# Global attention's output projection moved into the attention block, with its first groups loaded ahead and x added by matmul

## The chip, the cores and the metric

The kernel runs on one core of one Trainium2 chip. The metric is the device time of one execution in microseconds (us), lower is better. The kernel before is stated as the median of three runs.

## What is computed

A modulated transformer block on x of 2 x 2048 tokens with 256 channels. What matters here is the first half:

```python
h = _layernorm(x) * (1 + ca) + sa
x = x + ga * (h + attention(h) @ Wo.T)        # 8 heads of 32, causal, two softmaxes mixed
h = _layernorm(x) * (1 + cb) + sb             # input of the second half
x = x + gb * ffn(h)                           # two layers of local attention and feed-forward
```

`ga`, `ca`, `sa` and the others are vectors of 256, one for each of the two batches. The kernel computes the second line as `h*ga + x + o @ (Wo*ga)`, where `o` is the heads' output.

## The kernel before

The program is a row of blocks. Each has a list of instructions for every engine, and all engines meet at its end. The blocks are: setup, the q, k and v projections, the global attention (`attention_phase`), the output projection (`projection_phase`), and then twice local attention and feed-forward. Before a block with new semaphores, `prime` (lines 106 to 117) makes a small block of its own in which SyncE alone adds 1 to every semaphore, one instruction for each.

`attention_phase` goes through 16 turns, one for each batch and head (`BH = 16`). The normalised and modulated `h` lies in SBUF as `S.h1`, which shares its memory with `x3` (the trace calls it `x`). In a turn TensorE makes score tiles, takes row maxima from a transposed copy and multiplies the two sets of probabilities with the values (L757), ScalarE makes the exponentials, and VectorE the second set's exponents (L859, L865) and maxima. What follows a head is a chain of small steps over DRAM, which for heads 0 to 14 runs inside the next turn: ScalarE copies the last product out (`keep`, L796), SyncE sends it and the row sums (`send`, L551 and L552) and loads the sums turned (`sums_load`, L567), VectorE inverts them (`invert`, L876 and L878), SyncE stores and loads the shares (L573, L580), GpSimd weighs and adds (`normalise`, L677 and L681), and SyncE stores the head's output to `o_t` (`o_store`, L586). For head 15 there is no next turn: the chain stands alone at the end of the block. Heads 0 to 7 belong to the first batch, 8 to 15 to the second.

`projection_phase` (from line 979) handles the 4096 tokens in 8 groups of 512 (`GROUPS = 8`, 4 tiles of 128 each); groups 0 to 3 are the first batch. For each group n:

- SyncE loads x (`fetch_x`, L1010, 512 KB) and the heads' outputs (`fetch_o`, L1014, two of 256 KB), and stores the new x (`send`, L1018).
- VectorE multiplies `h` by `ga` (`gate_x`, L1102), and GpSimd adds x to it (`add_x`, L1060).
- TensorE multiplies: 4 tiles by 2 halves of the channels, 8 matmuls of 256 columns, each recorded as two instructions (L1090), into one of two buffers of PSUM.
- VectorE adds the product (`residual`, L1110), takes mean and variance (L230, L235) and adds epsilon (L1115). GpSimd raises to -1/2 (`scale`, L1064), VectorE makes the offset (`centre`, L1120), ScalarE normalises (L1044), VectorE modulates (`modulate`, L1124), and GpSimd adds the shift into `x2` (`shift`, L1068), the input of the second half.

TensorE may begin group n only when `residual(n-2)` is done, since there are two buffers. After its second group ScalarE issues `W.load_local`: 11 transfers of the local attention's weights and tables, 5.9 MB (L964 to L968). The local attention block begins, as all blocks, when every engine is through.

Of the kernel before, what the change touches and what calls it, by code (L numbers as in the profile page):

```python
# [15 lines left out]
P = 128  # L16
# [81 lines left out]
def allocators(nc, ctx, sems, prefix=""):  # L98

    def sb(name, shape, dt=F32):  # L100
        return ctx.enter_context(nc.sbuf_tensor(prefix + name, shape, dt))

    def ps(name, shape, dt=F32):
        return ctx.enter_context(nc.psum_tensor(prefix + name, shape, dt))

    def sem(name):
        return sems.enter_context(nc.semaphore(prefix + name))

    return sb, ps, sem
# [348 lines left out]
def attention_phase(nc, S, io):  # L458
# [35 lines left out]
    with ExitStack() as ctx:  # L494
        sb, ps, sem = allocators(nc, ctx, S.sems)
        q3, k3 = ([sb(f"{n}{s}", [ALLROWS, T], F32R) for s in range(SETS)] for n in ("q3_", "k3_"))
        geo, kp_t = sb("geo_rows", [P, 2, T]), sb("kp_t", [P, NT, BH])
        vx = [sb(f"vx_{s}", [P, NT, VW]) for s in range(SETS)]
        chunk_max, row_max = sb("chunk_max", [P, NT, NG]), sb("row_max", [P, NT])
        max_parts = sb("max_parts", [P, 2 * NT], F32R)  # L500
        max_rows = [sb(f"max_rows{p}", [2 * n, P], F32R) for p, (_, n) in enumerate(PARTS)]
        probs = sb("probs", [P, PSLOTS, 2, GTOK])
        mask_n, mask_t = sb("mask_n", [P, P], BF16), sb("mask_t", [P, P], BF16)
        later = sb("later", [P, P])

        share = sb("share", [P, H])
        out_t = sb("out_t", [P, 2, GTOK])
        raw = [sb(f"raw_{s}", [P, 2, GTOK]) for s in range(SETS)]
        shares = sb("shares_in", [P, 2, GTOK])
        sums = sb("sums_in", [P, T * 2 // P])  # L510
        summed = sb("summed", [P, GTOK])

        piece_lo, piece_hi = sb("piece_lo", [P, PIECE], F32R), sb("piece_hi", [P, PIECE], F32R)

        dots = geo[0:BH, :, :]
        top, low = (probs[0:BH, 2 * k:2 * k + 2, :, :].rearrange("h s k t -> h (s k t)") for k in range(2))
        geo_x = sb("geo_x", [P, GSLOTS, GTOK])
        a_ps = ps("a_ps", [P, ABANKS, 512])
        st_ps = ps("st_ps", [P, STBANKS, 512])
        o_ps = ps("o_ps", [P, 2, 512])  # L520
        turned_ps = st_ps[:, 0, 0:NT * BH].rearrange("p (t h) -> p t h", h=BH)
        names = ("setup a_ready a_used parts_ready values_in max_in st_ready st_used geo_ready geo_link probs_ready pv_done o_used max_chain "
                 "inverted shared weighed summed sums_in shares_out shares_in o_out piece_hi piece_lo piece_out cleared dots_in kp_turned kp_kept chain rows_out").split()
        q = {n: sem("t_" + n) for n in names}

        masks_in, max_out, piece_in = sem("t_masks_in"), sem("t_max_out"), sem("t_piece_in")
        loads = [sem(f"t_load{s}") for s in range(SETS)]
        out_sent = [sem(f"t_out_sent{k}") for k in range(2)]
        geo_in = [sem(f"t_geo_in{g}") for g in range(NG)]
        SETUP, CHAIN = 2 * SETS + 1, 5  # L530
        LOAD, SENT, OUT = 16 * 6, 16 * 3, 16 * NG

        PROBS0, ST0, PV0, O0 = GSLOTS - 1, STBANKS - 1, PSLOTS - 1, 1

        prime(nc, q | dict(enumerate((*loads, *out_sent, *geo_in))), (("probs_ready", PROBS0), ("st_used", ST0), ("pv_done", PV0), ("o_used", O0)))

        def chunk(c):
            return slice(c * GTOK, (c + 1) * GTOK)

        with nc.Block() as block:  # L540

            @block.sync
            def _(sp):
                def send(b, g, s):
                    evens = SENT * (NG // 2) * (b + 1) + START
                    sp.wait_ge(q["o_used"], b * NG + g + 1 + O0 + START)
                    for kind in range(2):
                        if kind and g == NG - 1:

                            sp.wait_ge(out_sent[0], evens)  # L550
                        sp.dma_start(raw[s][g * D:(g + 1) * D, kind, :], out_t[kind * HALF:kind * HALF + D, g % 2, :]).then_inc(out_sent[g % 2], 16)  # L551
                    sp.dma_start(S.sums[ds(b, 1), :, chunk(g)].rearrange("h k t -> (h k) t"),  # L552
                                 out_t[D:D + HALF + 1:HALF, g % 2, :]).then_inc(out_sent[g % 2], 16)

                def geo_load(b, g):

                    sp.wait_ge(q["geo_ready"], (b - 1) * NB + last_of_group[g] + 1 + START)
                    geo_fetch(b, g)

                def geo_fetch(b, g):  # L560
                    sp.dma_start(geo[:, :, chunk(g)], S.geo[ds(b, 1), :, chunk(g)].to_broadcast([P, 2, GTOK])).then_inc(geo_in[g], 16)

                def sums_load(b):
                    flat = S.sums.rearrange("b k (p n) -> (b k p) n", p=HALF)
                    first, sent = b * P, SENT * (NG // 2) * (b + 1) + START
                    sp.wait_ge(out_sent[1], sent)
                    sp.dma_start(sums[:, :], flat[ds(first, P), :]).then_inc(q["sums_in"], 16)  # L567

                def shares_store(b):
                    flat = S.shares.rearrange("b k (p n) -> (b k p) n", p=HALF)  # L570
                    first = b * P
                    sp.wait_ge(q["shared"], b + 1 + START)
                    sp.dma_start(flat[ds(first, P), :], sums[:, :]).then_inc(q["shares_out"], 16)  # L573

                def shares_load(b):
                    flat = S.shares.rearrange("b k (p n) -> (b k p) n", p=HALF)
                    first = b * P
                    sp.wait_ge(q["shares_out"], 16 * (b + 1) + START)
                    for g in range(NG):
                        sp.dma_start(shares[g * D:(g + 1) * D, :, :], flat[ds(first, P), :].rearrange("(k g p) n -> g k (p n)", k=2, g=NG)[g:g + 1].to_broadcast([D, 2, GTOK])).then_inc(q["shares_in"], 16)  # L580

                def o_store(b):
                    first = [b // H * (NG * H) + b % H + g * H for g in range(NG)]
                    sp.wait_ge(q["summed"], b + 1 + START)
                    for g in range(NG):
                        sp.dma_start(S.o_t[ds(first[g], 1), :, :].rearrange("h d t -> (h d) t"),  # L586
                                     summed[g * D:(g + 1) * D, :]).then_inc(q["o_out"], 16)
# [1381 lines left out]
```

## Time and profile before

| | |
|---|---|
| median of 3 runs | 2828.08 us (2824.79 to 2835.54) |
| the profiled execution | 2834.22 us, its span 2832.1 us |
| PE busy | 2550.9 us (90%) |
| DVE busy | 2193.7 us (77%) |
| ACT busy | 1558.2 us (55%) |
| POOL busy | 562.9 us (20%) |
| DMA | 204.92 MB, mean 72 GB/s |

PE is TensorE's matmuls, DVE VectorE, ACT ScalarE, POOL GpSimd and SP SyncE. Busy time is an average over all stages. The page also cuts the span into 40 slices of 70.8 us; in slices 17 and 18, which hold the end of the global attention and the projection, PE is busy for four and seven tenths, and nine nearly everywhere in the attention around them. What a change between two stages is worth is to be read from the instructions of that stretch in order of time.

### The profile page before, as it was taken

What the parts mean: (1) busy time and instruction counts of PE and PEld (TensorE: products, weight loads), DVE (VectorE), ACT (ScalarE), POOL (GpSimd) and SP (SyncE); (2) the same over time, 40 slices, a digit from 0 to 9 for tenths busy, and PEclk for the clock granted to TensorE, in tenths of its full rate; (3) what the DMA queues carried; (4) which work ended last, traced back from release to release, by engine and by line L of the source; (5) the groups of instructions that cost most, each with busy time, mean ns of one, the idle gap of its engine ahead of it and who ended that gap; (6) DMA issues with size and microseconds to landing.
All of it is one profiled execution on the core that took longest, in us unless ns stands there. A gap on an engine that the chain in (4) does not pass through costs nothing. (4 is left out here: it accounts for less than half of the span.)

```text
span 2832.1 us, 45352 instructions
## 1 busy us (share of the span) xinstructions
PE 2550.9 (90%) x14072; PEld 1543.8 (55%) x14072; DVE 2193.7 (77%) x4594; ACT 1558.2 (55%) x3447; POOL 562.9 (20%) x388
## 2 busy tenths in 40 slices
PE   4995999999999999954799999979979999997998
PEld 2443433333333333313577777758867777775877
DVE  4776999999999999957688888745657888885665
ACT  0221666676667666642466666634426666665443
POOL 0110011011111010116333333300013333331000
PEclk7997899999999999987799999989989999999999
DMA  2334254454554444417200000030020000001121
GB/s 87 113 113 123 79 143 125 106 132 115 132 137 117 116 122 126 114 52 253 63 10 9 8 9 9 17 121 21 12 56 10 9 8 9 9 20 34 49 65 40
DMA packets 123906, 204.92 MB, mean 72 GB/s; under 512 B 22560, under 2 KB 71008, under 8 KB 120400
## 3 DMA queue, kind: packets, MB, share of 16 engines
q1 hardware_dynamic: 109040, 163.96, 21.1%
q0 software_dynamic: 8832, 21.80, 2.7%
q10 hardware_dynamic: 5920, 17.75, 1.7%
q8 instruction: 58, 0.95, 0.1%
q14 instruction: 56, 0.46, 0.1%
HBM read 125.30 MB, written 54.26 MB: 63 GB/s over the span
## 5 line engine op out<-in xcount | busy, mean ns | idle before, releaser
L757 PE MATMUL o_ps<-probs,vx 128*33 128x512 f32 (+3 forms) x2560 | 546.6, 549 | 0.0
L808 ACT ACTIVATE probs<-st_ps 128x512 f32<-128x512 f32 (+3 forms) x640 | 339.2, 530 | 319.2 <-PE st_ps L742 181.7
L859 DVE SCALAR_TENSOR_TENSOR geo_x<-geo_rows,kp_t 128x512 f32<-128x512 f32 (+3 forms) x640 | 438.5, 709 | 3.7 <-ACT probs L810 3.7
L838 DVE TENSOR_REDUCE chunk_max<-a_ps 128x1 f32<-128x512 f32 (+3 forms) x640 | 359.1, 603 | 45.2 <-PE a_ps L725 37.1
L810 ACT ACTIVATE probs<-geo_x 128x512 f32<-128x512 f32 (+3 forms) x640 | 360.9, 564 | 12.7 <-DVE geo_x L865 12.7
L1256 PE MATMUL local_in_ps<-w_local,local_ht 128*128 128x512 f32 x1152 | 323.2, 418 | 9.6 <-ACT local_sq L1398 5.3
L1417 ACT ACTIVATE local_probs<-local_s_ps,local_bias,local_inv 128x256 f32<-128x256 f32 x512 | 282.6, 563 | 13.6 <-DVE local_bias L1512 13.5
L725 PE MATMUL a_ps<-k,q 96*128 96x512 f32 (+3 forms) x640 | 238.7, 447 | 43.4 <-DVE chunk_max L838 35.7
L1693 PE MATMUL ff_ag_ps<-ff_ht_parts,w 128*128 128x512 f32 (+1 forms) x1056 | 258.3, 403 | 20.1 <-DVE ff_gate L1802 11.9
L1424 ACT ACTIVATE local_pt<-local_pt_ps 128x512 f32<-128x512 f32 x256 | 152.4, 596 | 208.5 <-PE local_pt_ps L1314 200.3
L757 PEld LDWEIGHTS o_ps<-probs,vx 128*33 128x33 f32 x2560 | 124.4, 112 | 261.3 <-issue 187.0
L725 PEld LDWEIGHTS a_ps<-k,q 96*128 96x128 f32 x640 | 109.7, 199 | 265.9 <-DVE chunk_max L838 126.0
L1508 DVE TENSOR_REDUCE local_top<-local_s_ps 128x4 f32<-128x1024 f32 x128 | 156.8, 1225 | 121.1 <-PE local_s_ps L1300 121.1
L1256 PEld LDWEIGHTS local_in_ps<-w_local,local_ht 128*128 128x128 f32 x1152 | 208.5, 194 | 58.3 <-issue 18.7
L1693 PEld LDWEIGHTS ff_ag_ps<-ff_ht_parts,w 128*128 128x128 f32 (+1 forms) x1056 | 199.1, 191 | 74.4 <-DVE ff_gate L1802 19.8
L1519 DVE TENSOR_SCALAR local_probs<-local_probs,local_rden 128x256 f32<-128x256 f32 x512 | 223.0, 477 | 9.0
L1585 POOL TENSOR_TENSOR local_inv<-local_norm,half 128x16 f32<-128x16 f32 x64 | 186.5, 2915 | 176.4 <-DVE local_norm L1497 109.3
L740 PE MATMUL st_ps<-q,k 98*128 98x512 f32 (+3 forms) x640 | 218.4, 413 | 3.4 <-DMA q<-maxima 3.4
L1706 PE MATMUL ff_y_ps<-ff_w,ff_act_t 128*128 128x256 f32 x1152 | 147.5, 283 | 14.5 <-DVE ff_act_t L1808 13.8
L1324 PE MATMUL local_o_ps<-local_pt,local_v_ring 128*64 128x128 f32 x2048 | 154.6, 282 | 3.3 <-ACT local_pt L1424 3.1
L1314 PE MATMUL local_pt_ps<-ident,local_probs 128*128 128x128 f32 x1024 | 151.6, 282 | 6.4 <-DVE local_probs L1519 1.4
L1706 PEld LDWEIGHTS ff_y_ps<-ff_w,ff_act_t 128*128 128x128 f32 x1152 | 138.4, 188 | 21.2 <-DVE ff_act_t L1808 21.0
(171 smaller groups left out, 3850.2 us busy)
## 6 DMA issues: line engine op xcount, KB each, us to landing
geo_rows<-geo SPq DMA_DIRECT2D x64, 512.0 KB, 7.7
q<-q_parts SPq DMA_DIRECT2D x48, 256.0 KB, 4.2
k<-k_parts SPq DMA_DIRECT2D x48, 256.0 KB, 6.4
piece_lo<-in_pieces POOLq DMA_DIRECT2D x15, 768.0 KB, 5.5
weight_parts<-piece_hi SPq DMA_DIRECT2D x15, 768.0 KB, 3.4
weight_parts<-piece_lo SPq DMA_DIRECT2D x15, 768.0 KB, 6.0
raw<-out_t SPq DMA_DIRECT2D x128, 64.0 KB
shares_in<-shares SPq DMA_DIRECT2D x64, 128.0 KB, 4.7
```

The source lines that it names most:

```text
L725: ins = pe.matmul(slot[:, 0:width], q3[s][0:ROWS, it * P:(it + 1) * P], k3[s][0:ROWS, c * GTOK:c * GTOK + width], start=True, stop=not diag)
L740: ins = pe.matmul(out[:, off:GTOK], k3[s][:, j * P:(j + 1) * P], q3[s][:, g * GTOK + off:(g + 1) * GTOK], start=True, stop=not diag)
L757: ins = pe.matmul(o_ps[kind * HALF:kind * HALF + VW, g % 2, off:GTOK], vx[s][:, j, :], probs[:, i % PSLOTS, kind, off:GTOK], start=j == 0, ...
L808: act.activation(probs[:, s % PSLOTS, 0, off:GTOK], st_ps[:, (b * NB + s) % STBANKS, off:GTOK], ACT.Exp).then_inc(q["st_used"], 1)
L810: act.activation(probs[:, s % PSLOTS, 1, off:GTOK], geo_x[:, s % GSLOTS, off:GTOK], ACT.Exp).then_inc(q["probs_ready"], 1)
L838: dve.reduce_max(chunk_max[:, it, c:c + 1], a_ps[:, n % ABANKS, 0:width], AX.X).then_inc(q["a_used"], 1)
L859: ins = dve.scalar_tensor_tensor(out[:, off:GTOK], geo[:, 1, at], kp_t[:, j, ds(b, 1)].rearrange("p o -> p o"), geo[:, 0, at], ALU.add, AL ...
L1256: last = pe.matmul(in_ps[:, j, :], ht[:, p, a, k, :], w[:, b, k, j * INNER:(j + 1) * INNER], start=i == 0, stop=i == len(steps) - 1)
L1417: last = act.activation(probs[:, hd, :], s_ps[:, a, x % 2 * 2 * P:(x % 2 + 1) * 2 * P], ACT.Exp, bias=bias[:, hd:hd + 1], scale=inv[:, p, ...
L1519: last = dve.tensor_scalar(probs[:, hd, :], probs[:, hd, :], rden[:, hd:hd + 1], None, ALU.mult)
L1693: last = pe.matmul(ag_ps[0:rows, x % 2, half, :], w1[:, a, k, c0:c0 + rows], ht_parts[:, b, k, :], start=i == 0, stop=i == len(steps) - 1)
L1706: last = pe.matmul(y_ps[:, t, :], act_t[:, a, x, t * P:(t + 1) * P], w2[:, b, x, :], start=(x, i) == (0, 0), stop=x == HC - 1 and i == len ...
```

## The change

- `projection_phase` is gone. A class `Projection` holds its pieces, and `attention_phase` calls them at the end of each engine's list, in the same block. The semaphores of the projection and of the later stages are primed in the one `prime` ahead of the attention. Some buffers of the last chain and of the projection lie on the other side of SBUF (`Ahead`), so that they don't share memory with what the attention still uses.
- The projection's weights (now loaded twice, once for each batch, straight into `w_gated`) and x of group 0 are loaded at the attention's start, and the heads' outputs of groups 0 and 1 (first batch, complete since turn 8) when SyncE has finished its turns. x of group 1 follows `sums_load(15)`.
- VectorE gates the weights and h of groups 0 to 5 before `invert(15)`, and of groups 6 and 7 after it.
- x is added by TensorE: two matmuls of 512 columns with the identity open the accumulation of each group. `add_x` on GpSimd is gone.
- The offset is made by GpSimd (`centre * rstd`), with `centre = -mean` made by VectorE ahead of it, so one hand-over between the two is gone.
- The last head's chain is laced into it: on SyncE the group 2 loads stand ahead of `o_store(15)`, on GpSimd `scale(0)` stands ahead of `normalise(15)`.
- `W.load_local` stays on ScalarE after group 1.

The core of the diff:

```diff
+    values.close()
+    W = later_buffers(nc, S, ctx)
+    stage = Projection(nc, right, ahead, S, W, io)
+    primed = {"p_" + n: x for n, x in stage.q.items()} | {"l_" + n: x for n, x in S.local.items()} | {"f_" + n: x for n, x in S.ff.items()}
...
+            maxima_in(0, 0)
+            stage.fetch_w(sp)
+            stage.fetch_x(sp, 0, 0)
+            turns(sp, turn)
+            sp.wait_ge(q["o_out"], OUT * H + START)
+            for p in range(2):
+                stage.fetch_o(sp, p, p)
+            send(BH - 1, NG - 1, (BH - 1) % SETS)
+            sums_load(BH - 1)
+            sp.wait_ge(q["piece_out"], 16 * 2 * (BH - 1) + START)
+            stage.fetch_x(sp, 1, 1)
+            shares_store(BH - 1)
+            shares_load(BH - 1)
+            stage.next_group(sp, 2)
+            o_store(BH - 1)
+            stage.next_group(sp, 3)
+            for n in range(2):
+                stage.send(sp, n)
+            sp.wait_ge(q["o_out"], OUT * BH + START)
+            for n in range(GPB, GROUPS):
+                stage.next_group(sp, n)
+                stage.send(sp, n - 2)
+            stage.last_sends(sp)
...
+            pool.wait_ge(max_out, 16 * len(PARTS) * BH)
+            stage.gpsimd(pool, lambda: normalise(BH - 1, (BH - 1) % SETS))
...
+            pe.wait_ge(q["a_used"], len(ORDER) + START)
+            stage.tensor(pe)
...
+            act.wait_ge(q["piece_out"], 16 * 2 * (BH - 1) + START)
+            stage.scalar(act)
...
+            dve.wait_ge(q["piece_out"], 16 * 2 * (BH - 1) + START)
+            stage.gate_weights(dve)
+            stage.gate(dve, 0, GROUPS - 2)
+            invert(BH - 1)
+            stage.gate(dve, GROUPS - 2, GROUPS)
+            stage.vector(dve)
```

And in the class:

```diff
+    def next_group(self, sp, n):
+        sp.wait_ge(self.q["mm_done"], n - 1 + START)
+        self.fetch_x(sp, n, n % 2)
+        self.fetch_o(sp, n, n % 2)
...
+        def scale(n, p):
+            pool.wait_ge(q["var"], n + 1 + START)
+            pool.tensor_tensor(self.rstd[:, p, :], self.rstd[:, p, :], self.S.half[:, 0:GT], ALU.pow).then_inc(q["rstd"], 1)
+            pool.wait_ge(q["rstd"], n + 1 + START)
+            pool.tensor_tensor(self.offset[:, p, :], self.centre[:, p, :], self.rstd[:, p, :], ALU.mult).then_inc(q["offset_ready"], 1)
...
+        scale(0, 0)
+        between()
+        scale(1, 1)
+        shift(0, 0)
+        for n in range(1, GROUPS - 1):
+            scale(n + 1, (n + 1) % 2)
+            shift(n, n % 2)
+        shift(GROUPS - 1, 1)
...
+            pe.wait_ge(self.x_in[p], 16 * (n // 2 + 1) + START)
+            pe.wait_ge(q["x1_ready"], n - 1 + P0 + START)
+            for t in range(0, GT, 2):
+                pe.matmul(self.y_ps[:, p, t:t + 2, :], self.S.ident[:, :], self.xin[p][:, t:t + 2, :], start=True, stop=False)
+            pe.wait_ge(self.o_in[p], 16 * CC * (n // 2 + 1) + START)
...
+        residual(0, 0)
+        dve.memset(self.S.x2[:, 0, :], 0.0)
+        dve.memset(self.S.x2[:, XS, :], 0.0)
+        with dve.Fori(0, GROUPS // 2 - 1) as i:
+            for p in range(2):
+                n = 2 * i + p
+                residual(n + 1, 1 - p)
+                modulate(n, p)
+        residual(GROUPS - 1, 1)
+        modulate(GROUPS - 2, 0)
+        modulate(GROUPS - 1, 1)
```

## Rows read from the trace of the kernel before

**Rows 1.** Busy per stretch: us, PE, PEld, DVE, ACT, POOL, PEclk, DMA share, GB/s

```profile
1244.40:1277.00 32.60, 0.06 (x1) 0.07 (x1) 4.60 (x8) 0.55 (x1) 5.70 (x3) 0.55 0.28 87
...
1301.00:1318.00 17.00, 0.39 (x3) 0.16 (x1) 16.25 (x30) 4.15 (x8) 11.83 (x7) 0.64 0.98 374
```

**Rows 2.** Timeline of the attention's end: start, us, engine, line, operation [idle before]

```profile
1239.85 0.29 DVE L865 TENSOR_TENSOR geo_x<-geo_x,later 128x128 f32<-128x128 f32 x1
...
1241.95 2.35 PE L757 MATMUL o_ps<-probs,vx 128*33 128x512 f32 x16
...
1249.37 0.35 DVE L876 RECIPROCAL sums_in<-sums_in 128x32 f32<-128x32 f32 x1 [9.23 <-DMA sums_in<-sums]
...
1250.03 0.35 SPq L573 DMA_DIRECT2D shares<-sums_in  x1
...
1255.91 2.34 POOL L677 TENSOR_TENSOR raw<-raw,shares_in 128x1024 f32<-128x1024 f32 x1 [20.80 <-DMA shares_in<-shares]
1258.33 1.26 POOL L681 TENSOR_TENSOR summed<-raw 128x512 f32<-128x512 f32 x1
1259.62 1.73 SPq L586 DMA_DIRECT2D o_t<-summed  x4
```

**Rows 3.** The priming block's instructions (line 117) between attention and projection

```profile
L117 PEldq DRAIN  x1: 13/13/13, 1265.4 to 1265.4; - x1
L117 SPq DRAIN  x1: 7/7/7, 1269.9 to 1269.9; - x1
```

**Rows 4.** Timeline of the projection's first groups and of a group at full pace

```profile
1276.94 9.61 PE L1090 MATMUL y_ps<-w_gated,ot 128*128 128x256 f32 x32 [32.64 <-DMA ot<-o_t]
...
1283.24 1.22 DVE L1110 TENSOR_TENSOR x<-x,y_ps 128x1024 f32<-128x1024 f32 x1 [9.00 <-PE y_ps L1090]
...
1288.39 1.22 DVE L1110 TENSOR_TENSOR x<-x,y_ps 128x1024 f32 x1
1288.51 2.08 ACT L1044 ACTIVATE normed<-x,offset,rstd 128x256 f32<-128x256 f32 x4 [43.56 <-DVE offset L1120]
...
1291.51 0.17 DVE L1115 TENSOR_SCALAR rstd<-mv 128x4 f32<-128x4 f32 x1
...
1292.54 3.72 PE L1090 MATMUL y_ps<-w_gated,ot 128*128 128x256 f32 x16 [2.03 <-DMA ot<-o_t]
...
1296.22 1.21 DVE L1110 TENSOR_TENSOR x<-x,y_ps 128x1024 f32 x1
```

**Rows 5.** GpSimd and VectorE side by side: durations of L1064, then timeline

```profile
L1064 POOL TENSOR_TENSOR rstd<-rstd,half x8: 1018/1984/2049, 1286.6 to 1343.1; 128x4 f32<-128x4 f32 x8
...
1291.70 1.23 DVE L1124 TENSOR_TENSOR normed<-normed,mod 128x1024 f32<-128x1024 f32 x1
1291.75 2.04 POOL L1064 TENSOR_TENSOR rstd<-rstd,half 128x4 f32<-128x4 f32 x1 [0.78 <-DVE rstd L1115]
...
1293.78 2.49 POOL L1068 TENSOR_TENSOR x<-normed,mod 128x1024 f32 x1
1293.98 2.32 DVE L1120 SCALAR_TENSOR_TENSOR offset<-mv,rstd 128x4 f32<-128x4 f32 x1
```

**Rows 6.** DMA issues from 1284 to 1290 us: KB each, median us from issue to landing

```profile
x_again<-in_x SPq DMA_DIRECT2D x1, 512.0 KB, 5.3
```

**Rows 7.** The weight loads' issue and what waited behind them (timeline; landing of L1010)

```profile
1296.34 0.93 ACTq L964 DMA_DIRECT2D w_local<-weight_parts  x2
...
1303.61 1.53 ACTq L968 DMA_DIRECT2D wo_local<-in_pieces  x1
...
DMA to landing us min/median/max: 16.3/16.3/16.3
...
1317.84 13.47 PE L1090 MATMUL y_ps<-w_gated,ot 128*128 128x256 f32 x48 [16.61 <-DMA ot<-o_t]
```

**Rows 8.** The projection's last group and the local attention's first matmul (timeline)

```profile
1339.74 1.21 DVE L1110 TENSOR_TENSOR x<-x,y_ps 128x1024 f32<-128x1024 f32 x1
...
1353.60 0.66 PE L1244 MATMUL local_in_ps<-ident,mod 128*128 128x128 f32 x2 [22.29 <-PEq L1003]
```

More of the change, by code:

```diff
@@ new lines, with __init__ @@
+class Ahead:
+    def __init__(self, nc, ctx):
+        sb, _, _ = allocators(nc, ctx, ctx)
+        self.out_t = sb("out_t", [P, 2, GTOK], side="right")
+        self.raw = [sb(f"raw_{s}", [P, 2, GTOK], side="right") for s in range(2)]
+        self.shares = sb("shares_in", [P, 2, GTOK], side="right")
+        self.sums = sb("sums_in", [P, T * 2 // P], side="right")
+        self.summed = sb("summed", [P, GTOK], side="right")
+        self.share = sb("share", [P, H], side="right")
+        self.w_gated = sb("w_gated", [P, B, CC, C], side="right")
+        self.ot = sb("ot", [P, 2, CC, GTOK], side="right")
+        self.x_first = sb("x_again_first", [P, GT, C], side="right")
@@ L460, in attention_phase @@
+def attention_phase(nc, S, io, ctx, values):
     NG = NT // GT
@@ L923 @@
-P0 = 1
-PRIMES = (("l_p_done", P0), ("l_pv_done", P0), ("f_act_done", P0), ("f_act_lo", P0), ("p_x2_done", P0), ("p_x1_ready", P0), ("p_normed", P0))
+    right = ExitStack()
+    ahead = Ahead(nc, right)
+    sb, ps, sem = allocators(nc, values, S.sems)
+    q3, k3 = ([sb(f"{n}{s}", [ALLROWS, T], F32R) for s in range(SETS)] for n in ("q3_", "k3_"))
+    geo, kp_t = sb("geo_rows", [P, 2, T]), sb("kp_t", [P, NT, BH])
+    vx = [sb(f"vx_{s}", [P, NT, VW]) for s in range(SETS)]
+    chunk_max, row_max = sb("chunk_max", [P, NT, NG]), sb("row_max", [P, NT])
@@ new lines, in attention_phase @@
+    max_parts = sb("max_parts", [P, 2 * NT], F32R)
+    max_rows = [sb(f"max_rows{p}", [2 * n, P], F32R) for p, (_, n) in enumerate(PARTS)]
+    probs = sb("probs", [P, PSLOTS, 2, GTOK])
+    mask_n, mask_t = sb("mask_n", [P, P], BF16), sb("mask_t", [P, P], BF16)
+    later = sb("later", [P, P])
+    share, out_t, raw, shares, sums, summed = ahead.share, ahead.out_t, ahead.raw, ahead.shares, ahead.sums, ahead.summed
+    piece_lo, piece_hi = sb("piece_lo", [P, PIECE], F32R), sb("piece_hi", [P, PIECE], F32R)
@@ new lines, in attention_phase @@
+    q = {n: sem("t_" + n) for n in names}
+    masks_in, max_out, piece_in = sem("t_masks_in"), sem("t_max_out"), sem("t_piece_in")
+    loads = [sem(f"t_load{s}") for s in range(SETS)]
+    out_sent = [sem(f"t_out_sent{k}") for k in range(2)]
+    geo_in = [sem(f"t_geo_in{g}") for g in range(NG)]
+    SETUP, CHAIN = 2 * SETS + 1, 5
+    LOAD, SENT, OUT = 16 * 6, 16 * 3, 16 * NG
+    PROBS0, ST0, PV0, O0 = GSLOTS - 1, STBANKS - 1, PSLOTS - 1, 1
+    values.close()
+    W = later_buffers(nc, S, ctx)
```

966 lines of the change are left out of this document (443 added, 523 removed).

## The prediction

> **What bounds the kernel now.** The busy shares of the page name TensorE, but its 40 slices show that it does not bound the stretch between the global attention and the local attention. So I read that stretch as busy time per window, then in order of time. From 1244.4 to 1277 us TensorE does next to nothing, at a granted clock of 0.55, and from 1301 to 1318 nothing again [rows 1]. In order of time there are four pieces.
> 1. TensorE's last product of the attention ends at 1244.3 (1241.95 + 2.35) and VectorE's last exponent at 1240.1. The last head's chain (sums, inversion, shares, two GpSimd steps, store) then runs alone until its store is issued at 1261.35 (1259.62 + 1.73) [rows 2].
> 2. The block ends, and SyncE primes alone from 1265.4 to 1269.9 [rows 3]. The projection's first loads start cold, its first product at 1276.94, and `residual(0)` at 1283.24 [rows 4].
> 3. A group then takes 7.8 us (`residual(1)` starts at 1288.39, `residual(2)` at 1296.22). TensorE needs only 3.72 us of it; VectorE and GpSimd fill the rest, partly by standing in each other's way [rows 4, 5].
> 4. The weight loads, issued from 1296.34 to 1305.14, hold back what is queued beside them: x of group 5 took 16.3 us to land, and groups 5 to 7 started only at 1317.84 [rows 7]. The DMA engines were 0.98 busy at 374 GB/s [rows 1].
> The last `residual` begins at 1339.74 and the local attention's first matmul at 1353.60, 13.9 us later [rows 8]. From the end of the attention's matmuls that is 109.3 us, of which eight groups at 3.72 us of TensorE are 30. All of the change is in there, but for what it moves to the attention's start.
>
> **Part by part.** I follow the new order of time, by the durations of this execution.
>
> *Priming.* The projection's block primes 78 semaphores in 4.5 us [rows 3]. One fewer is needed now, but the others move to the block before the attention, where every engine waits for SyncE too. Nothing is hidden: plus 4.5 us there. What is gained is the pause around the block, which I count in the times below.
>
> *Loads at the attention's start.* 1 MB and three issues (some 1.3 us of SyncE at 0.4 to 0.5 each, by the last head's issues) stand behind `maxima_in(0, 0)`. I take 0; if the row maxima of head 0 come behind them, it costs 1 MB at 374 GB/s, 3 us at most [rows 1].
>
> *Gates under the chain.* VectorE is free from 1240.1 and must invert at 1249.37 [rows 2]. Two gated weights (512 columns each, half of a 1.23 us step of 1024 [rows 5]) and six gates of 1.23 make 8.6 us, so they end at 1248.7: hidden, 0.7 to spare. Groups 6 and 7 follow the inversion, so VectorE is ready for `residual(0)` at about 1252.4.
>
> *Group 0 on TensorE.* x and weights have long been there, and the heads' outputs are asked for at 1237, after the last turn's store. A group now has two more matmuls of 512 columns. I take them at the cost of the columns of L1090: 3.72 us / 8 is 0.465 for 256, so 1.86 for both, 5.6 us a group. Bounds: 0 (if the records' fixed part were all) to 3.7 at the lower clock. TensorE goes on at once at full clock: group 0 is done at 1249.9. Group 1 waits for its x, issued at 1248.1 and landed after 5.3 us [rows 6], and ends near 1258. So `residual(0)` starts at 1252.4 instead of 1283.24, and `residual(1)` at 1258.
>
> *The chain beside it.* From `residual` to its variance 3.3 us passes (1288.39 to 1291.68 [rows 4]), and one more small step makes it 3.5. `scale(0)` waits for that until 1255.9, takes 1.02 and the new offset multiply. No row shows a GpSimd multiply of 4 columns. Its bounds are the square of nothing and the 1.02 us of the power; the two long ones (2.34 for 1024, 1.26 for 512 [rows 2]) leave 0.2 at no columns, and I take 0.2. `normalise(15)` stands behind it in GpSimd's order and so starts at 1257.4 instead of 1255.9; `o_store(15)` is issued from 1261.2 to 1263. Group 3's loads stand behind it on SyncE and land near 1269. `residual(2)` comes at 1264 (its loads go out before the store), `residual(3)` at 1273 to 1276.
>
> *The weight loads.* They follow `normalise(1)` on ScalarE. Its offset is made after `normalise(15)`, near 1264, so it ends at 1266, and the issues keep ScalarE until 1275 (8.8 us as before). Group 4's loads wait for the heads' last store and go out at 1265.2 to 1266.6. So they meet the weights, in the place where group 5's did before: 2 MB of stores and loads in SyncE's queue and 5.9 MB in ScalarE's. Before, all drained in 21.5 us (1296.3 to 1317.8 [rows 7]). Here there are some 11 MB from 1263.5 on, at 374 GB/s 29 us, to 1293. Group 4 lands between 1276 and 1287, group 5 near 1290, and with 5.6 us on TensorE, partly done by then, `residual(5)` starts at 1294.
>
> *The pace behind that.* VectorE per group: 3.5 + 1.23. The gate is gone, and the offset step, which took 2.32 us because GpSimd's shift was running [rows 5]. GpSimd: power, multiply, shift, with the power held while VectorE modulates. In sum 5.2 us, less than TensorE's 5.6. So 5.6 to 6 a group, and `residual(7)` starts near 1306. After it 3.9 to the variance, 1.2 to modulate group 6, 1.2 for power and multiply, 2.34 for the shift of group 6, 1.23 and 2.34 for group 7 make 12.3: the local attention starts at 1318.5 instead of 1353.6.
>
> [...]
>
> *Sum.* 1353.6 - 1318.5 = 35.1 gained, 4.5 paid at the start: 30.6 us. The profiled execution took 2834.2 us (span 2832.1), which gives 2803.6; it lies 6.1 us over the median of 2828.08, so against the median it is 2797.5. The rest of the kernel is unchanged in work and order.
>
> **The rivals.**
> - *Weights slow only themselves.* For it: the group loads stand earlier in their queue than the weights, and 1 MB needs under 3 us alone. Against it: x of group 5 before, issued just behind the first weights, took 16.3 us [rows 7]. Then `residual(4)` still waits for ScalarE's issues (`normalise(2)` ends at 1277, then modulate), starts at 1278.4, and three groups at 5.6 put `residual(7)` at 1295.2: 11 us less, 2786.5.
> - *TensorE becomes the bound.* It would wait for each load in turn and run at the lower level of its clock (0.55 of full was granted while it idled [rows 1]; the first two groups took 9.61 against 7.44 [rows 4]). A group then costs up to 10.3 us, since it has 40% more columns than before. If that holds for groups 3 to 7 behind the weights, `residual(7)` is 15 us later: 2812. By the rule of the Trainium skill (TensorE: Matmul & The Clock Gate) the array runs at half rate after idling, so waits for loads would be paid twice; this chip's rows agree (0.55).
> - *The overlap doesn't happen.* If TensorE or VectorE gets through its own tail late, because the heads' outputs of groups 0 and 1 (1 MB ahead of the last send in SyncE's queue) hold up the last head, only the block's end and the shorter step remain: at most 4.1 us from the last store's issue to the priming (1261.35 to 1265.4 [rows 2, 3]) and 7 groups by 1 us, less the 0 that moving the priming costs in sum. Half of the first and the second make 9 us, less up to 3 us of the start's loads: 2822.
> - *The turns get longer.* `values` and the attention's buffers now lie elsewhere in SBUF, and more code hangs on the block. From the first scores at 291 to 1244 a turn takes 59.6 us, sixteen times. If each loses 1.9 us the gain is gone; above 2.8 us a turn the kernel is slower by over 0.5%. At 3 us it is 2797.5 + 48 = 2845. Against it: no instruction inside a turn is added, moved or made to wait, and VectorE, TensorE and ScalarE keep their order.
>
> **How the numbers follow.** Forecast, weights in the way: 0.52, 2797.5, itself from 2791 to 2805 (group 4 landing 6 us earlier or later). Weights harmless: 0.2, 2786.5. TensorE bound: 0.16, 2812. No overlap: 0.08, 2822. Longer turns: 0.04, 2845. The range from 2784 to 2813 holds the first three but their edges. A measurement of this kernel can tell 0.5% (14 us) from no change, so faster is under 2813.9: 0.52 + 0.2 + most of 0.16, 0.87. Same: 0.09. Slower: 0.04.
>
> **What would show it.** Right: the local attention's first matmul 70 to 80 us after the attention's last (109 before), `residual(0)` near 8 us after it; a priming of 6.8 us before the attention; one long wait of TensorE for the outputs of group 4 or 5, ending 25 us after the weights' first issue; GpSimd's second small step near 0.2 us. Wrong: turns that last over 60 us, `w_gated` landing late, or ScalarE's issues running into `normalise(3)`.

## The result, and the profile after

| | before | after |
|---|---|---|
| median of 5 runs | 2830.08 us (2824.79 to 2835.54) | 2811.63 us (2810.55 to 2816.78) |
| the profiled execution | 2834.22 us, span 2832.1 | 2816.78 us, span 2814.8 |
| attention's last matmul ends | 1244.3 | 1249.4 |
| from there to the local attention's first matmul | 109.3 us | 86.1 us |
| from that to the end of the span | 1478.5 us | 1479.4 us |

The ratio is 0.9941 (0.9926 to 0.9956): faster by 18.5 us (0.6%), where 30.6 had been forecast. The time, 2811.6, lies inside the range and is 14 us above the predicted 2797.5.

The table closes: 23.2 us gained between attention and local attention, 5.1 paid before (3.3 of them by the first scores, 1.7 within the attention), 0.9 after it, in sum 17.3 us of span. 35.1 and 4.5 had been forecast. So the question is where 11.9 us of the stretch went.

First, the timeline of the changed kernel, from the attention's last product to the first groups (start, us, engine, line, operation; in brackets the idle time before it and what ended it):

```profile
1247.02 2.35 PE L956 MATMUL o_ps<-probs,vx 128*33 128x512 f32 x16
...
1249.30 1.98 PE L563 MATMUL y_ps<-x_again_first,ident 128*128 128x512 f32 x4
...
1251.12 3.62 PE L567 MATMUL y_ps<-w_gated,ot 128*128 128x256 f32 x16
...
1254.51 0.35 DVE L1079 RECIPROCAL sums_in<-sums_in 128x32 f32<-128x32 f32 x1 [1.37 <-DMA sums_in<-sums]
...
1257.20 1.98 PE L563 MATMUL y_ps<-x_again,ident 128*128 128x512 f32 x4 [2.46 <-DMA x_again<-in_x]
1257.27 2.99 SPq L765 DMA_DIRECT2D shares_in<-shares  x4
1257.53 1.22 DVE L598 TENSOR_TENSOR x<-x,y_ps 128x1024 f32<-128x1024 f32 x1
```

The overlap is there. Group 0 runs on TensorE the moment the last product is done, the identity's two matmuls and the products cost 1.98 + 3.62 = 5.6 us, and `residual(0)` starts 8.2 us after the attention's last matmul (38.9 before). VectorE had 1.37 us to spare ahead of the inversion: the six gates cost nothing there.

Then the same timeline for group 2 and around the weight loads:

```profile
1264.94 3.25 PE L563 MATMUL y_ps<-x_again_first,ident 128*128 128x512 f32 x4 [2.31 <-DMA x_again_first<-in_x]
...
1267.98 4.09 PE L567 MATMUL y_ps<-w_gated,ot 128*128 128x256 f32 x16
...
1268.70 0.92 ACTq L1169 DMA_DIRECT2D w_local<-weight_parts  x2
...
1272.15 1.02 SPq L493 DMA_DIRECT2D x_again_first<-in_x  x1
1273.22 8.42 SPq L497 DMA_DIRECT2D ot<-o_t  x2
...
1281.42 1.22 DVE L598 TENSOR_TENSOR x<-x,y_ps 128x1024 f32 x1 [4.62 <-PE y_ps L567]
...
1293.70 3.77 PE L563 MATMUL y_ps<-x_again_first,ident 128*128 128x512 f32 x4 [12.46 <-DMA x_again_first<-in_x]
...
1297.27 4.79 PE L567 MATMUL y_ps<-w_gated,ot 128*128 128x256 f32 x16
...
1302.28 1.22 DVE L598 TENSOR_TENSOR x<-x,y_ps 128x1024 f32 x1 [16.32 <-PE y_ps L567]
...
1307.42 1.22 DVE L598 TENSOR_TENSOR x<-x,y_ps 128x1024 f32 x1 [0.61 <-PE y_ps L567]
...
1318.16 1.22 DVE L598 TENSOR_TENSOR x<-x,y_ps 128x1024 f32<-128x1024 f32 x1 [1.01 <-PE y_ps L567]
```

x of group 4, issued at 1272.15, came 21.4 us later. TensorE waited 12.46 us for it, and VectorE 16.32 us for TensorE. It is the collision of [rows 7], one group earlier. SyncE spent 8.42 us in issuing two transfers that took it 0.98 at 1260.77. Busy time per stretch (us; PE, PEld, DVE, ACT, POOL with instructions; granted clock; DMA share; GB/s):

```profile
1282.00:1294.00 12.00, 0.29 (x1) 0.30 (x2) 3.83 (x14) 3.20 (x7) 4.47 (x3) 0.67 1.00 372
1294.00:1302.00 8.00, 8.00 (x21) 5.20 (x21) 0.00 (x0) 0.00 (x0) 0.00 (x0) 0.65 0.70 254
```

While TensorE waited, the DMA engines were wholly busy at 372 GB/s and its granted clock fell to 0.67 of full (a mean over the stretch); at 0.65 group 4 then took 3.77 + 4.79 = 8.6 us instead of 5.6. Group 2 had been slow in the same way: behind a wait of 2.31 us it took 7.1 us, from 1264.94 to 1272.07, and the granted clock from 1264.9 to 1272.1 was 0.76. Behind group 4, at a granted clock of 1.00, the `residual` steps came 5.14 to 5.5 us apart, down from 7.8.

Last, the end of the block: the timeline, then the instructions of line 725, where the block ends (durations min/median/max in ns, first and last start).

```profile
1327.34 2.34 POOL L545 TENSOR_TENSOR x<-normed,mod 128x1024 f32<-128x1024 f32 x1 [1.25 <-DVE normed L609]
...
1335.44 0.66 PE L1287 MATMUL local_in_ps<-ident,mod 128*128 128x128 f32 x2 [17.38 <-PEq L725]
```

```profile
L725 POOLq DRAIN  x1: 7847/7847/7847, 1327.3 to 1327.3; - x1
...
L725 SPq DRAIN  x1: 193/193/193, 1327.4 to 1327.4; - x1
```

The last work ends at 1327.34 + 2.34 = 1329.7, SyncE had been ready since 1327.6, and yet the local attention starts at 1335.4. GpSimd's DRAIN ran to 1335.2, 5.5 us beyond its last operation. A DRAIN is the instruction with which an engine closes its list in a block; the block ends when all of them are through. GpSimd's also stood in the trace of before, at the end of the attention's block; my argument had passed over it. These are the same views of before:

```profile
L540 POOLq DRAIN  x1: 6609/6609/6609, 1258.5 to 1258.5; - x1
...
L540 SPq DRAIN  x1: 7/7/7, 1262.9 to 1262.9; - x1
```

```profile
L1003 POOLq DRAIN  x1: 2448/2448/2448, 1350.9 to 1350.9; - x1
```

There GpSimd's last addition ended at 1259.6 [rows 2] and its drain at 1265.1, again 5.5 us later. The old projection block, in which GpSimd issued no transfer, ended with a drain of 2.45 us, which is its last shift and nothing more.

Two other blocks of the kernel before show what these 5.5 us go with. In the q, k and v projections (L267) GpSimd issued 8 transfers of 512 KB, in the local attention (L1224) 2:

```profile
L267 POOLq DRAIN  x1: 1664/1664/1664, 215.5 to 215.5; - x1
...
L1224 POOLq DRAIN  x2: 3197/3200/3203, 1831.6 to 2568.8; - x2
```

Their last operations ended at 216.42 and 1834.55, so the drains ran 0.75 and 0.26 us beyond them. In the attention, with 66 transfers, it was 5.47 us. All 14 traces of this study agree, wherever no transfer of GpSimd's was still under way: less than 0.1 us with no transfer since the last drain, 0.24 to 0.26 with 2, 0.74 to 0.75 with 8, 5.47 to 5.48 with 66. That is about 0.08 us for each transfer, and it follows neither their bytes (the 8 large ones cost 0.75) nor the number of GpSimd's operations (96 in the local attention, 48 in the attention of before).

In numbers relative to the attention's last matmul, forecast and measured: `residual(0)` 8.1 and 8.2, `residual(1)` 13.7 and 13.4, `residual(2)` 19.7 and 22.9, `residual(3)` 29 to 32 and 32.1, `residual(5)` 49.7 and 58.1, `residual(7)` 61.7 and 68.8, last shift's end 74.0 and 80.3, local attention 74.2 and 86.1. So the weights took 7.1 us more than forecast, the block's end 5.6 more (5.8 from the last shift to the first matmul, instead of 0.2), and the tail 0.8 less: 11.9 in sum.

### The profile page after: what moved, and what is told of

It reads as the page before. It is cut to its first block and busy times, and to the rows that moved or that the text cites. A ratio compares the mean times of both kernels' runs of the same rounds, so it can differ in the third digit from the quotient of the medians.

```text
span 2814.8 us, 45277 instructions
## 1 busy us (share of the span) xinstructions
PE 2567.7 (91%) x14104; PEld 1550.8 (55%) x14104; DVE 2177.7 (77%) x4594; ACT 1558.7 (55%) x3447; POOL 542.6 (19%) x388
## 5 line engine op out<-in xcount | busy, mean ns | idle before, releaser
L1736 PEld LDWEIGHTS ff_ag_ps<-ff_ht_parts,w 128*128 128x128 f32 (+1 forms) x1056 | 199.7, 192 | 74.2 <-DVE ff_gate L1845 19.1
L1299 PEld LDWEIGHTS local_in_ps<-w_local,local_ht 128*128 128x128 f32 x1152 | 207.8, 193 | 58.1 <-issue 18.7
```

The source lines that it names most:

```text
L1299: last = pe.matmul(in_ps[:, j, :], ht[:, p, a, k, :], w[:, b, k, j * INNER:(j + 1) * INNER], start=i == 0, stop=i == len(steps) - 1)
L1736: last = pe.matmul(ag_ps[0:rows, x % 2, half, :], w1[:, a, k, c0:c0 + rows], ht_parts[:, b, k, :], start=i == 0, stop=i == len(steps) - 1)
```

## The experiments

Theory A was: GpSimd's drain holds the block's end, and the lump of weights holds groups 4 to 7. All kernels are the changed kernel with the edit shown. Ratios are against the kernel before, whose median beside them was 2830.6 us in the first four, 2827.7 in the next four, 2837.9 in three, and 2838.4 in the last. Moments are us after the attention's last matmul, and "lag" is the time from the last shift's end to the local attention's first matmul.

**1. GpSimd drained earlier, where it idles.**

```diff
             pool.wait_ge(max_out, 16 * len(PARTS) * BH)
+            pool.drain()
             stage.gpsimd(pool, lambda: normalise(BH - 1, (BH - 1) % SETS))
```

> The changed kernel with one drain instruction on GpSimd after its last turn, where it idles. In the changed kernel the block ends 5.6 us after GpSimd's last shift (1329.68 to 1335.3), as the attention block before ended 5.5 us after GpSimd's last add. Theory A, GpSimd's drain pays once for the transfers that it issued in the block: the drain moves under the last head's chain and the local attention starts within 0.5 us of the last shift, so about 5.4 us less than the changed kernel (2806). Theory B, the 5.6 us come at every end of a block with a long list on GpSimd, whatever was drained: the end still takes 5.6 us, and the time is that of the changed kernel (2811.6).

2807.9 us, 0.9926 (0.9904 to 0.9948). In the time the step of 5 us is within the intervals; the trace shows it. Timeline, and lines 725 and 905 of this kernel:

```profile
1323.87 2.34 POOL L545 TENSOR_TENSOR x<-normed,mod 128x1024 f32<-128x1024 f32 x1 [1.26 <-DVE normed L609]
...
1326.57 0.66 PE L1288 MATMUL local_in_ps<-ident,mod 128*128 128x128 f32 x2 [11.98 <-PEq L725]
```

```profile
L725 POOLq DRAIN  x1: 2445/2445/2445, 1323.8 to 1323.8; - x1
...
L905 POOLq DRAIN  x1: 7126/7126/7126, 1235.6 to 1235.6; - x1
```

The lag fell from 5.8 to 0.36 us with `residual(7)` at 68.8 in both. The early drain (L905) ran from 1235.6 to 1242.7, beside VectorE's and TensorE's last steps; GpSimd's last operation ahead of it had ended at 1237.2, so it is the same 5.5 us, moved to where they cost nothing. They belong to what GpSimd did before and are not paid twice.

**2. The weight loads behind the last group.**

```diff
-        self.W.load_local(act, self.S, self.io, 0)
         with act.Fori(1, GROUPS // 2) as i:
             for p in range(2):
                 normalise(2 * i + p, p)
+        self.W.load_local(act, self.S, self.io, 0)
```

> The changed kernel with the local attention's weight loads (5.9 MB) issued after the last normalised group instead of after the second. Theory A, the weights hold back group 4: its x lands 5 us after its issue instead of 21.4, TensorE's wait of 12.5 us and its slow group 4 are gone, and residual(7) starts 50 to 54 us after the attention's last matmul instead of 68.8. The weights then land 20 us after their issue, so the local attention waits for its tables, and 8 to 12 us of the 17 come back. Theory B, group 4 waits for something else in SyncE's queue (the stores of groups 0 and 1 ahead of it): residual(7) stays at 65 us or later, and the kernel is 10 us slower than the changed one.

2804.7 us, 0.9907 (0.9885 to 0.9928). `residual(7)` came at 52.9 instead of 68.8, the local attention at 71.1 instead of 86.1. Timeline, and a stretch of busy times as above:

```profile
1283.42 1.22 DVE L598 TENSOR_TENSOR x<-x,y_ps 128x1024 f32 x1 [5.81 <-PE y_ps L567]
1288.62 1.22 DVE L598 TENSOR_TENSOR x<-x,y_ps 128x1024 f32 x1 [0.67 <-PE y_ps L567]
```

```profile
1288.00:1305.00 17.00, 16.44 (x62) 11.24 (x61) 13.30 (x43) 6.27 (x12) 14.53 (x12) 1.00 0.78 249
```

Groups 4 to 7 pass at 5.1 to 5.7 us, at full clock, with TensorE busy for 16.44 of 17 us. So the lump costs 16 us of `residual(7)` in that place, but the local attention then waits for its tables (VectorE 4.3 us for `qk_scale`), and the weights' landing eats part of the gain.

**3. The weight loads ahead of the first group's normalise** (`W.load_local(act, S, io, 0)` just before `stage.scalar(act)`, and gone from its place).

> The changed kernel with the same weight loads issued as soon as the attention's last product is copied out, 19 us earlier. Theory A, the weights delay whatever is loaded beside them: x of group 1, the shares and group 2 come late (10 us or more until residual(1)), and groups 4 to 7 then run at 5.2 to 5.6 us each; residual(7) starts 60 to 66 us after the attention's last matmul, a gain of 3 to 8 us over the changed kernel. Theory B, that small transfers of the last head suffer most: the store of the last head lands 20 us later and the kernel is slower than the changed one by 5 us or more.

2809.8 us, 0.9934 (0.9909 to 0.996): no difference from the changed kernel. Now x of group 1 came late (TensorE waited 13.7 us) and the last head's sums (VectorE 11.7 us), `residual(0)` fell back from 8.2 to 18.4, and `residual(7)` came at 65.6, the local attention at 82.9. The lump delayed what stood beside it in this place too.

**4. The priming on four engines.**

```diff
-        @block.sync
-        def _(sp):
-            for name, s in sems.items():
-                sp.sem_inc(s, START + extra.get(name, 0))
+        for k, engine in enumerate((block.sync, block.scalar, block.vector, block.gpsimd)):
+
+            @engine
+            def _(eng, k=k):
+                for name, s in items[k::4]:
+                    eng.sem_inc(s, START + extra.get(name, 0))
```

> The changed kernel with the 116 semaphores primed by four engines side by side instead of by SyncE alone. In the changed kernel the priming takes 6.7 us (249.7 to 256.4), before it took 2.3 us there. Theory A, priming costs 58 ns each and nothing hides it: 1.7 to 2 us instead of 6.7, so 4.7 us less in all. Theory B, the attention's start is bound by the loads of q and k (landed near 269) that began before: nothing is gained.

2807.2 us, 0.9924 (0.9904 to 0.9943). In the trace the priming ahead of the attention went from 6.7 us (249.7 to 256.4) to 2.2 to 2.7 (249.4 to 251.6 and 252.1), and the first scores from 294.95 to 290.77 (291.61 in the kernel before). The stretch after the attention was that of the changed kernel (86.4). The cost at the start is the priming alone, and four engines take it off.

**5. The weights in pieces.** ScalarE's loop is written out; one table and scale go behind each of groups 2 to 5, the big weights behind group 6.

```diff
-        self.W.load_local(act, self.S, self.io, 0)
-        with act.Fori(1, GROUPS // 2) as i:
-            for p in range(2):
-                normalise(2 * i + p, p)
+        for n in range(2, GROUPS):
+            normalise(n, n % 2)
+            if n < 6:
+                self.W.load_table(act, self.S, self.io, 0, n - 2)
+            if n == 6:
+                self.W.load_products(act, self.S, self.io, 0)
```

> The changed kernel with the weight loads in pieces on ScalarE: one table with its scales after each of groups 2 to 5, the products' weights (3.6 MB) after group 6. With the loads all at the end residual(7) started 52.9 us after the attention's last matmul instead of 68.8, but the local attention's first rotation then waited for its tables, 16.7 us after the block's start instead of 9.2. Theory A, the loads hurt by standing in a lump beside the group loads, and there is room between: residual(7) at 53 to 57 us, the first rotation 9 to 12 us after the local attention's start, in all 12 to 16 us less than the changed kernel. Theory B, any byte of them beside the groups delays the groups as much as it takes itself (2.1 MB at 374 GB/s, 6 us, for the tables): residual(7) at 59 us or later.

2794.8 us, 0.988 (0.9864 to 0.9897). `residual(7)` 54.8, local attention 72.0, and VectorE's first rotation of the local attention at 81.5 (95.3 in the changed kernel, 87.9 in experiment 2). It keeps 14 of the 16 us, and the first rotation shows nothing paid later: the same bytes, in another order.

**6. Experiments 1, 4 and 5 together.**

> The changed kernel with the weight loads in pieces, GpSimd's drain under the last head's chain and the priming on four engines. If the three effects lie in different places (4.6 us of priming, 5.4 of drain, 12 to 16 of weights) they add up to 22 to 26 us less than the changed kernel, 2786 to 2790. If the drain was hidden by something else that comes late, some 5 us of it are missing.

2789.5 us, 0.9876 (0.9853 to 0.9898), a ratio that can't be told from that of 5. `residual(7)` 53.5, local attention 70.3: better than in 5, but the lag, now 5.4 us, is back. SyncE's timeline, and line 727 (the block's end):

```profile
1295.77 9.70 SPq L1208 DMA_DIRECT2D mod<-x  x1
...
1306.82 1.96 SPq L1208 DMA_DIRECT2D mod<-x  x1
```

```profile
L727 POOLq DRAIN  x1: 2445/2445/2445, 1301.7 to 1301.7; - x1
...
L727 SPq DRAIN  x1: 187/187/187, 1309.0 to 1309.0; - x1
```

GpSimd is done at 1304.1, as in 1. Now SyncE is last, at 1309.2: it issues the local attention's first tiles behind its stores, one small load took 9.70 us to issue, and the last issue ended at 1308.8. It did not wait for the stores: the last of them had landed at 1305.4.

**7. x added by GpSimd, as before the change.** The matmuls by the identity are gone; GpSimd adds x to the gated product.

```diff
-            for t in range(0, GT, 2):
-                pe.matmul(self.y_ps[:, p, t:t + 2, :], self.S.ident[:, :], self.xin[p][:, t:t + 2, :], start=True, stop=False)
...
+        def add_x(n):
+            pool.wait_ge(self.x_in[n % 2], 16 * (n // 2 + 1) + START)
+            pool.wait_ge(q["x_gated"], n + 1 + START)
+            pool.tensor_tensor(self.x1(n), self.x1(n), self.xin[n % 2][:, :, :], ALU.add).then_inc(q["x_added"], 1)
```

> The changed kernel with one part undone: x is added by GpSimd as before (8 adds of 2.35 us), the 16 matmuls with the identity are gone, and x of a group is asked for when the add two groups earlier is done. Theory A, GpSimd is the dearer place, since it and VectorE exclude each other: the last three groups come 6.5 to 7.5 us apart instead of 5.2 to 5.6, and the kernel is 2 to 6 us slower than the changed one. Theory B, TensorE is what counts in the long wait (group 4 took 8.6 us at a granted clock of 0.65, 3.8 of them for x): the kernel is up to 4 us faster.

2810.9 us, 0.9942 (0.9922 to 0.9961). VectorE's timeline behind the weights, one `residual` per group:

```profile
1299.56 1.21 DVE L606 TENSOR_TENSOR x<-x,y_ps 128x1024 f32 x1
...
1306.41 1.21 DVE L606 TENSOR_TENSOR x<-x,y_ps 128x1024 f32 x1
```

6.85 us a group instead of 5.14 to 5.5: the matmuls by the identity do shorten a group, by about 1.5 us. In the whole it cost 2.1 us of the local attention's start (88.2) and nothing that the time can tell, because `residual(4)` waits for group 4's loads in either kernel (52.5 here, 52.9 there) and only the groups behind it run at their own pace.

**8. The gates in the loop again,** gates 0 and 1 behind the inversion and one more beside each group.

```diff
-            stage.gate(dve, 0, GROUPS - 2)
             invert(BH - 1)
-            stage.gate(dve, GROUPS - 2, GROUPS)
+            stage.gate(dve, 0, 2)
...
+                dve.tensor_tensor(self.x1(n + 2), self.x1(n + 2), self.mod(n + 2, 2), ALU.mult).then_inc(q["x_gated"], 1)
                 residual(n + 1, 1 - p)
```

> The changed kernel with another part undone: only two gates of h ahead of the groups (behind the inversion), the others in the loop as before, 1.2 us each on VectorE. Theory A, VectorE was the bound of a group and the moved gates are the gain: the last three groups come 6.3 us apart or more instead of 5.2 to 5.6, 2 to 4 us slower in all. Theory B, since the offset step left VectorE it has 1.2 us to spare in each group: no change of more than 1 us between the attention's last matmul and residual(7).

2804.5 us, 0.9921 (0.9896 to 0.9947), the pace 5.0 to 5.6 us, `residual(7)` at 65.7, the local attention at 83.0, like the changed kernel's second execution (9). Moving the gates brought nothing that can be seen. In the changed kernel VectorE waited 0.61 to 0.67 us for TensorE in a group, so the room is half of the 1.2 us expected; a gate of 1.2 us fills it, and the two groups behind one came 5.6 us apart in place of 5.2.

**9. The changed kernel once more, beside the next two.**

> The changed kernel itself once more, beside these. It was 0.9941 (0.9926 to 0.9956) of the kernel before; the same is expected, 2810 to 2813, residual(7) 68 to 70 us after the attention's last matmul and the local attention's first matmul 86 us after it. The time of the attention itself (first score to last product) is expected anywhere from 948 to 957 us, as in the seven profiles so far: by theory A (turns unchanged) no trend against the 952.7 of the kernel before, by theory B (buffers placed elsewhere make turns longer) 955 or more.

2817.2 us, 0.9926 (0.9902 to 0.9949). The ratio repeats. In this execution `residual(7)` came at 66.0 and the local attention at 83.2, and the attention itself took 965.8 us from its first scores (954.4 in the first profile, 952.7 in the kernel before). Group 4's x landed at 41.8 in place of 44.2, which is most of the difference in `residual(7)`. Over all kernels of this study the attention took 947.6 to 967.9, without order by kernel: the two longest (9 and 12) were measured beside a kernel before that took 2838. That much noise of one execution is why the stretch is read here and not the span.

**10. The first tiles' loads ahead of the last stores** (6, with `load_tile` before the two last `send`).

> The kernel with all three remedies (weights in pieces, drain under the chain, priming on four engines), whose block still ended 5.4 us after GpSimd's last shift, because SyncE's last issue of the local attention's first tiles took 9.7 us beside the weights and SyncE came through at 1309.0. Here SyncE loads these tiles before its last two stores. Theory A, SyncE's issues in the full queue are what is late: the block ends within 1 us of the last shift, 4 to 5 us less than all three (2789.5), near 2785. Theory B, the weights late in the block cost the same wherever the issue stands (the tiles or tables land late): the local attention's first rotation stays 41.8 us after the start of residual(5) or later, and the time does not move.

2799.4 us, 0.9875 (0.9838 to 0.9912). The lag stayed (4.4), which neither theory had. The tiles' loads were issued by 1304.7, but the two last stores now stood behind them and beside the weights' large part: they took SyncE 7.13 us to issue, the last one landed at 1320.1, and SyncE waited for it. In 6 the issues of the tiles had been last, here the landing of the stores is: the edit put one late thing in place of the other.

**11. As 10, with group 3's loads ahead of the last head's store.**

```diff
-            o_store(BH - 1)
             stage.next_group(sp, 3)
+            o_store(BH - 1)
```

> The same, and group 3's loads are issued before the store of the last head (o_store(15)) instead of after it. With the weights out of the way residual(2) and residual(3) were still 10.2 us apart, at a pace of 5.2 for the next ones. Theory A, group 3 waits for its own loads, which stand behind a store that has nothing to do with it: issued at 14 instead of 18.5 us, residual(3) 4 to 5 us earlier, and the whole row behind it by 2 to 5. Theory B, group 4 must wait for that store in any case, and comes no earlier: residual(4) moves by less than 1 us, and the time with it.

2791.0 us, 0.9848 (0.9815 to 0.988). `residual(3)` 25.9 (30.2 in 10), `residual(7)` 52.8 (55.2 in 10), local attention 68.6. TensorE gets group 3 some 4 us earlier, and 2.4 us of that reach `residual(7)`. The waits of SyncE show what is last now (us in total, times, longest):

```profile
SPq L727 <- DMA x<-x: 13.6, 1, 13.6
```

**12. As 11, with the wait for the stores moved** out of the block, to VectorE before it clears the buffer that reuses their memory in the local attention.

```diff
-        sp.wait_ge(self.q["x1_out"], 16 * GROUPS + START)
...
                 if layer == 0:
+                    dve.wait_ge(S.x1_out, 16 * GROUPS + START)
                     dve.memset(S.x3[:, 0, :], 0.0)
```

> The last kernel (weights in pieces, drain under the chain, priming on four engines, tiles and group 3 early), and the wait for the stores of x moves from SyncE at the block's end to VectorE in the local attention, ahead of its first write into that memory, 9 us later. In the last two kernels the block ended 4.4 us after GpSimd's last shift, and SyncE's own wait named the stores (13.6 us). Theory A, this wait was all that was late: the local attention's first matmul comes within 0.6 us of the last shift, 3.5 to 4 us less than before, a ratio of 0.983 to 0.984 to the kernel before. Theory B, the weights' lump behind group 6 is what is late, and VectorE now waits instead: the first rotation stays 77 to 78 us after the attention's last matmul.

2794.1 us, 0.984 (0.9817 to 0.9863), against a kernel before of 2838.4: the lowest ratio, though not to be told from those of 10 and 11 by their intervals. Its timeline:

```profile
1319.82 2.34 POOL L547 TENSOR_TENSOR x<-normed,mod 128x1024 f32<-128x1024 f32 x1 [1.16 <-DVE normed L611]
...
1322.51 0.66 PE L1301 MATMUL local_in_ps<-ident,mod 128*128 128x128 f32 x2 [11.88 <-PEq L727]
```

0.35 us of lag. The local attention starts 62.9 us after the attention's last matmul (86.1 in the changed kernel, 109.3 before), and its first rotation comes at 72.2. By its ratio this version takes 1.6% (44 us) off the kernel before; the change as it stood took 0.6% to 0.7%.

## Why the prediction was right and wrong

**Held, as worked out.** Priming: 6.7 us before the attention where it had been 2.3, 4.4 more for the 4.5 forecast. The first scores came 3.3 later, and experiment 4 shows that this is the priming; the other 1.7 of the 5.1 us lie within the attention, inside what it varies by. The 1 MB loaded at the attention's start cost nothing to be seen. The gates fitted under the last head's chain (0.7 us to spare forecast, 1.37 found). `residual(0)` and `residual(1)` were within 0.3 us, the second by luck: an issue at 1248.1, 5.3 us to land and 5.6 us on TensorE make 1259, not the 1258 of the forecast, and the load landed after 3.9 us. The identity's matmuls, priced by columns at 1.86 us, took 1.98 at first; the group 5.6. GpSimd's small multiply took 0.20 us, as the two long rows had given. The tail after `residual(7)` was 11.5 us for 12.3. The power still took 1.92 to 1.98 us beside VectorE's tensor_tensor and 1.04 alone, so [rows 5] carried over. The Trainium skill (SBUF — State Buffer, SBUF: two separate sides) gives the exclusive hold on the port shared with GpSimd to VectorE instructions with two SBUF inputs, as this tensor_tensor has; the trace agrees.

**Failed: the block's end.** The step from the last shift to the local attention was put at 0.2 us, from the end of the old projection block, and the 4.1 us between the last store's issue and the priming were counted as saved. They were not all pause. GpSimd's drain ended 5.5 us after its last addition (L540), and for the last 2.2 us of it SyncE had stood ready. The change does not remove this work: it moves it behind the projection, where nothing hides it. That is 5.6 of the 11.9 us, shown by experiment 1, which hides it and wins back 5.4. The mistake was to take the price from the old projection block (L1003), in which GpSimd had issued nothing, instead of from a block in which it had issued the same 66 transfers.

**Mis-sized: the weights.** The mechanism was right, and in the right group. The step that failed is the landing of group 4: it was put in the middle of the crowd, between 32 and 43 us after the attention, and TensorE could begin it only at 44.3, with the crowd's end (DMA share 1.00 until 1294, 0.70 behind it), though its x had been issued only 3.5 us after the first weights. The sum for `residual(5)`, 49.7, let TensorE be through with group 4 before group 5 landed, and so needed group 4 by 38.5, two groups of 5.6 earlier; 5.8 us are the later landing. Another 3.0 are the rival "TensorE becomes the bound", behind the weights in a single group instead of in five: after waiting 12.46 us group 4 ran at clock 0.65 (8.6 us for 5.6). The faster pace (5.14 to 5.5 us, forecast 5.6 to 6) gave back 0.4 up to `residual(5)`, which so was 8.4 late, and another 1.3 up to `residual(7)`, 7.1 late. By the Trainium skill (TensorE: Matmul & The Clock Gate, What's actually happening) the array runs at half rate after idling; the trace agrees for groups 2 and 4 (0.76 and 0.65), and shows the groups behind group 4 at full clock. (That rival's "40% more columns" was a slip: by the prediction's own 5.6 against 3.72 us it is 50%.) Experiments 2 and 5 show that all of this is the lump: 16 and 14 us of `residual(7)` go with it. By the Trainium skill (DMA: Bandwidth & Descriptors, Issuing engines are not separate DMA queues) transfers of different issuing engines interleave on the same DMA engines; the traces agree, and 16 us of `residual(7)` is what it cost here.

**Small.** `residual(2)` came 3.2 us late. About half is the start: the last head's four loads of shares kept SyncE 2.99 us (1.74 before), and group 2's loads stood behind them. The other half is the clock: group 2 took 7.1 us for 5.6. By `residual(3)` it had been caught up in the store's wait.

**The rivals.** "Weights slow only themselves" is refuted (21.4 us of landing); experiment 5 came near its time by an edit (`residual(7)` at 54.8, by that rival 50.9). "The overlap doesn't happen" is refuted by the first timeline. "The turns get longer" has nothing for it: attention took 954.4 us, 952.7 before, within what it varies by anyway. The range held the time, but only since the clock's rival had been let in; the main forecast's own 2791 to 2805 did not, and the drain that took a good part of the difference stood in no rival, so that is luck. With the drain counted, the forecast for the profiled execution would have been 2809.2, for 2816.8 measured.

**Left open.** What GpSimd does in the 5.5 us of its drain is not shown, and no run changed the number of its transfers alone; that they cost 0.08 us each is read across blocks. With a transfer of its own still under way it is longer: the last block's drain (L1644 in the kernel before, 8 transfers) took 5.86 us and ended at 2808.4, 0.4 us after the last of them landed. Nor is it shown why group 4's x took 21.4 us to land in one execution and 20.4 in the other.

## What to carry to other kernels

When a change merges or removes a block, list what each engine does at the old block's end (the drains of its line, with the gap between an engine's last operation and its drain's end) and ask where each goes; GpSimd, where it had issued transfers, paid about 0.08 us there for each, and could be drained earlier where it idled. Put large loads for a later stage in pieces between the loads of the present one, not in one lump: against no weights beside the groups (2), `residual(7)` came 2 us later with them in pieces (5) and 13 to 16 later with the lump. After each edit ask what is last now: with the weights in pieces the block's end was held in turn by GpSimd's drain (5), SyncE's issues (6) and the landing of the last stores (10, 11), and the drain's 5.4 us showed again only in 12, when the others were gone.

## What the runs showed of the hardware that I had not expected

- GpSimd's drain at the end of the block in which it had issued 66 transfers lasted 5.5 us beyond its last operation, in both kernels; with 8 it was 0.75 (L267), with 2 0.26 (L1224), and without any less than 0.1 (L1003).
- Two issues on SyncE took 8.42 us in a crowded queue (0.98 at 1260.77 in a quiet one), and a single one 9.70 in experiment 6; what stood behind it on SyncE waited as well.
- 512 KB landed after 5.3 us on a quiet queue [rows 6], after 16.3 [rows 7] and 21.4 us beside 5.9 MB on another engine's queue.
